# Second attention of a six-stage transformer kernel: GpSimd adds the key halves for all eight heads, and half of the output path moves by a slot

## The chip, the cores and the metric

The kernel runs on one core of one Trainium2 chip. The metric is the device time of one execution in microseconds (us). All of it is one launch; inputs and output lie in HBM.

## What is computed

The reference passes x (16 batches x 256 tokens x 128 channels, fp32) through six residual stages: a mixture-of-experts feed-forward, a grouped-query attention, the first feed-forward again, a routed feed-forward, a latent attention, and the routed feed-forward again. The change lies in the fifth, the second attention. Cut to what matters:

```python
c_q, c_kv = h_t @ W_DQ + b_DQ, h_t @ W_DKV + b_DKV      # 32 channels each
q = concat(c_q @ W_UQ + b_UQ, c_q @ W_QR + b_QR)        # 8 heads x (128 + 32)
k = concat(c_kv @ W_UK + b_UK, h_t @ W_KR + b_KR)
attn = softmax(q @ k.T / sqrt(160))                     # 256 x 256, per batch and head
out = (attn @ (c_kv @ W_UV + b_UV)) @ W_O + b_O
x = x + out                                             # h_t is layernorm(x)
```

## The kernel before

Each engine has its own hand-written list of instructions, and semaphores tie the lists together; the order inside a list never changes at run time. The functions `a1_pe`, `a1_act`, `a1_dve` and `a1_pool` issue the second attention for TensorE, ScalarE, VectorE and GpSimd. The first three loop over slots i = -2 to 15, and a slot has eight steps m = 0 to 7. In slot i three batches are in work at once:

- batch i + 2 is projected (`project`, lines 1139 to 1142, step 0), its keys are built by `head_keys` in two rounds of two (steps 2 and 4 on TensorE, lines 1158/1159), each copied to a rounded part by ScalarE (line 1315) and finished by VectorE (line 1397, one step later than the copy). TensorE's first round waits for VectorE's `low_inputs` (line 1386) and `vals` (line 1380). The second round reuses the same two PSUM banks and waits for VectorE's finished first round (semaphore kp_lo).
- batch i + 1 (from step 5 on, i + 2) gets its row maxima: in every step TensorE writes one bank of scores (`scores`, line 1176) and VectorE reduces it (`smax`, line 1404). There are two banks, so the scores of step m wait for the reduction of step m - 2.
- batch i gets its transposed scores (`scores_t`, line 1186) and exponentials (`exps`, ScalarE, line 1322). PT holds the exponentials: u = 0 for heads 0 to 3 (steps 0 to 3), u = 1 for heads 4 to 7 (steps 4 to 7), each with two halves of 128 keys.

The output path of a batch starts with `values(b, g)` (line 1201): 16 matmuls for the four heads of group g, two key halves each, into columns 0 to 255 of PSUM bank 6 + g. Beside it the sums over the keys go to columns 256 to 511 by matmuls with a block of ones (`sums`, line 1210). For g = 0 GpSimd first adds the two key halves (`pair`, line 1115, into PAIR), so that eight matmuls do; for g = 1 TensorE adds them with sixteen:

```python
if g:
    sums(b, g, (PT[:, g, 0, :, :], PT[:, g, 1, :, :]))
```

Then ScalarE copies the bank (`out_sums`, line 1328), TensorE turns it (`turn`, line 1221), VectorE divides (`normalise`, lines 1428/1429), TensorE turns both groups back (`back`, line 1227), ScalarE copies (`turned`, line 1333), TensorE projects out (`project_out`, line 1234), VectorE adds to the residual (`add`, line 1436) and takes the statistics (`stats`, lines 251/254), GpSimd makes the power (`next_power`, lines 261/263), VectorE normalises for the next stage (`normed`, line 270), TensorE turns it (`next_turn`, line 1243) and ScalarE copies it (`next_copy`, line 1337). VectorE's `maxima` (lines 1413 to 1416) packs the maxima of batch i + 1, TensorE turns them (line 1166), and VectorE's `shift` (line 1421) puts them into the queries. GpSimd also adds a bias to the residual (`bias`, line 1110).

Before the change slot i holds on TensorE: `turn(i-1, 0)` in step 0, `values` and sums of (i-1, 1) in step 1, `next_turn(i-2)` and `turn(i-1, 1)` in step 3, `values(i, 0)` and `back(i-1)` in step 5, the sums of (i, 0) and `maxima` in step 6, `project_out(i-1)` in step 7. A steady slot is one with all parts, i = 2 to 13: twelve of them.

## Time and profile before

| what | value |
|---|---|
| median of 3 runs (lowest, highest) | 1474.72 us (1471.44, 1475.7) |
| the profiled execution: its own time | 1477.36 us |
| its span, first to last instruction | 1475.6 us |
| TensorE matmul busy over the span | 1419.6 us (96%) |
| VectorE, ScalarE, GpSimd busy | 1113.8, 977.2, 633.1 us |
| mean granted TensorE clock | 0.99 |

Times in the trace count from the start of the span. A matmul row gives a modelled end, which overlaps the next one's start; the distance from start to start is what a group of matmuls costs. The twelve steady slots of the second attention lie from 1116.1 to 1285.9 us. Where a row merges several instructions (x16), its time is that of the whole group.

### The profile page before, as it was taken

How to read it: one execution, taken by the hardware profiler on the slowest of the kernel's cores; microseconds unless marked ns; L12 is line 12 of the kernel's file. 1: busy time of each engine (PE TensorE's matmuls, PEld its weight loads, DVE VectorE, ACT ScalarE, POOL GpSimd, SP SyncE). 2: the span in 40 equal slices, each digit the busy share in tenths (PEclk: the TensorE clock that was granted, in tenths of full speed). 3: DMA queues.
4: the chain of work that ended last, by engine and by line, in shares of the span. 5: the costliest groups of instructions: out<-in, count | busy, mean ns of one | idle time of the engine just before them, and what ended most of it. 6: DMA issues, size and time to landing. Idle time of an engine off the chain costs nothing.

```text
span 1475.6 us, 27285 instructions
## 1 busy us (share of the span) xinstructions
PE 1419.6 (96%) x9576; PEld 1146.5 (78%) x9576; DVE 1113.8 (75%) x2433; ACT 977.2 (66%) x1759; POOL 633.1 (43%) x596
## 2 busy tenths in 40 slices
PE   6999999989999999999999998999989999989998
PEld 6888888865666665688888876999967777769998
DVE  3766767688888889476777787687788898956765
ACT  5556656647777777755666567777746667657886
POOL 4466667610000000016666666677613233256664
PEclk8999999999999999999999999999999999989999
DMA  6000000000000000020000002000000000000001
GB/s 181 1 1 1 1 0 2 1 1 1 1 1 1 1 1 1 1 88 1 1 0 1 1 0 87 1 1 2 1 1 2 2 1 2 2 1 2 16 16 30
DMA packets 13319, 16.85 MB, mean 11 GB/s; under 512 B 768, under 2 KB 10496, under 8 KB 12928
## 3 DMA queue, kind: packets, MB, share of 16 engines
q1 hardware_dynamic: 13184, 15.11, 3.3%
q8 instruction: 77, 1.26, 0.3%
q14 instruction: 58, 0.48, 0.1%
HBM read 13.01 MB, written 2.10 MB: 10 GB/s over the span
## 4 chain that ended last, share of the span: by engine, by line
PE 84%; DVE 9%; ACT 3%; issue 2%; DMA 1%; POOL 0%; SPq 0%; DVEq 0%; POOLq 0%; ACTq 0%
PE PS L646 20%; PE PS L674 10%; PE PS L1835 9%; PE PS L1852 8%; PE PS L799 5%; PE PS L819 5%; PE PS L807 4%; PE PS L1201 2%; PE PS L778 2%; PE PS L1176 2%; PE PS L1210 2%; PE PS L1186 2%; PE PS L170 1%; PE PS L1158 1%; PE PS L1234 1%
## 5 line engine op out<-in xcount | busy, mean ns | idle before, releaser
L543 POOL TENSOR_TENSOR RR<-AR,RR 128x512 fp32r<-128x512 f32 x150 | 193.7, 1291 | 470.6 <-ACT RR L574 464.2
L610 ACT ACTIVATE AR<-PS 128x512 f32<-128x512 f32 x224 | 134.1, 599 | 164.7 <-PE PS L646 162.5
L512 DVE TENSOR_TENSOR AR<-AR,PS 128x512 f32<-128x512 f32 x224 | 153.4, 685 | 116.4 <-PE PS L646 113.7
L918 ACT ACTIVATE AR<-PS 128x512 f32<-128x512 f32 x256 | 152.4, 604 | 85.7 <-PE PS L807 85.0
L995 DVE TENSOR_REDUCE AR<-PS 128x2 f32<-128x512 f32 x256 | 172.2, 685 | 21.4 <-PE PS L799 20.6
L646 PE MATMUL PS<-XHI,WG 128*128 128x512 f32 x448 | 177.1, 395 | 0.0
L646 PE MATMUL PS<-XHI,WU 128*128 128x512 f32 x448 | 174.8, 390 | 0.9 <-DVE AR L512 0.7
L516 DVE TENSOR_TENSOR AR<-AR,PS 128x512 f32<-128x512 f32 x224 | 154.0, 687 | 8.1 <-POOL RR L543 0.5
L1835 PE MATMUL PS<-XHI,SL 128*128 128x256 f32 x576 | 135.0, 290 | 3.6 <-DVE XTR L2000 1.9
L2105 POOL CAST SL<-ZW 128x1024 fp32r x96 | 100.0, 1042 | 86.2 <-PE PS L1852 85.6
L1928 ACT ACTIVATE PS<-PS 128x1024 f32<-128x1024 f32 x96 | 96.9, 1009 | 59.5 <-PE PS L1835 59.2
L1835 PE MATMUL PS<-XLO,SL 128*128 128x256 f32 x576 | 133.9, 287 | 1.6 <-DVE XTR L2000 1.3
L799 PE MATMUL PS<-XLO,XHI 128*128 128x512 f32 x256 | 129.3, 505 | 3.0 <-DVE AR L995 2.4
L674 PE MATMUL PS<-RR,WD 128*128 128x512 f32 x450 | 126.5, 390 | 1.2 <-POOL RR L543 1.2
L2000 DVE SCALAR_TENSOR_TENSOR XTR<-PS,AR,RR 128x512 fp32r<-128x512 f32 x128 | 90.1, 746 | 45.5 <-ACT RR L1938 45.4
L1852 PE MATMUL PS<-XTR,SL 128*128 128x256 f32 x640 | 124.1, 284 | 0.3 <-DVE XTR L2000 0.3
L543 POOL TENSOR_TENSOR H<-AR,H 128x512 fp32r<-128x512 f32 x74 | 95.6, 1291 | 52.8 <-ACT H L574 50.8
L1322 ACT ACTIVATE AR<-PS 128x512 f32<-128x512 f32 x128 | 76.7, 603 | 46.8 <-PE PS L1186 46.1
L2103 POOL CAST SL<-ZW 128x1024 fp32r x96 | 99.9, 1041 | 16.4 <-DVE IDX L1764 6.8
L1852 PE MATMUL PS<-RR,SL 128*128 128x256 f32 x512 | 103.4, 285 | 2.3 <-DVE AR L1719 2.3
L1835 PEld LDWEIGHTS PS<-XHI,SL 128*128 128x128 f32 x576 | 100.6, 193 | 4.8 <-issue 3.8
L807 PE MATMUL PS<-XHI,XLO 128*128 128x512 f32 x256 | 102.9, 403 | 0.9 <-ACT AR L918 0.7
(284 smaller groups left out, 3510.0 us busy)
## 6 DMA issues: line engine op xcount, KB each, us to landing
X<-in_x SPq DMA_DIRECT2D x4, 512.0 KB, 6.5
out_x<-X SPq DMA_DIRECT2D x4, 512.0 KB, 3.5
AR<-in_w SPq DMA_DIRECT2D x1, 1792.0 KB, 11.7
XT<-in_w SPq DMA_DIRECT2D x1, 1608.0 KB, 6.3
AR<-in_zone_up SPq DMA_DIRECT2D x6, 256.0 KB, 5.2
AR<-in_zone_down SPq DMA_DIRECT2D x6, 256.0 KB, 6.1
XT<-in_sel SPq DMA_DIRECT2D x1, 896.0 KB, 6.5
SM<-in_small SPq DMA_DIRECT2D x1, 857.5 KB, 7.0
```

The costliest lines, as they stand in the source:

```text
L512: v.tensor_tensor(PRD[:, m % 2, :], SIL[:, m % 2, :], bank(2 + m % 2), ALU.mult).then_inc(S.prod, 1)
L516: v.tensor_tensor(GAT[:, m % 2, :], PRD[:, m % 2, :], bank(4 + m // SHARED), ALU.mult).then_inc(S.gated, 1)
L543: g.tensor_tensor(HL[k % 3], GAT[:, m % 2, :], HH[k % 3].bitcast(F32), ALU.subtract).then_inc(S.h_lo, 1)
L610: act.activation(SIL[:, m % 2, :], bank(m % 2), ACT.Silu).then_inc(S.silu, 1)
L646: last = pe.matmul(out, w[i][:, m * P:(m + 1) * P], x[:, bass.ds(c * 512, 512)], start=(j == 0), stop=(j == 2))
L674: last = pe.matmul(bank(6), WD[i][:, m, :], h[k % 3], start=(m == 0 and j == 0), stop=(m == MT0 - 1 and j == 2))
L799: pe.matmul(bank(m % 2), QS0[b % 3][:, j * SEQ + k * P:j * SEQ + (k + 1) * P], KS0[b % 3][:, 2 * gp:2 * gp + 2, :], start=True, stop=True) ...
L807: pe.matmul(bank(2 + m % 2), KS0[b % 3][:, g, k * P:(k + 1) * P], QS0[b % 3][:, jp * 512:(jp + 1) * 512], start=True, stop=True).then_inc( ...
L918: act.activation(PT[:, g % 2, k, 2 * jp:2 * jp + 2, :], bank(2 + m % 2).rearrange("p (j q) -> p j q", j=2), ACT.Exp, scale=SC0).then_inc(S ...
L995: v.tensor_reduce(MX[:, 2 * m:2 * m + 2], bank(m % 2).rearrange("p (h k) -> p h k", h=2), AX.X, ALU.max)\
L1835: last = pe.matmul(o, SL[:, k, 0, i, m * P:(m + 1) * P], x[:, b * SEQ:(b + 1) * SEQ], start=(j == 0), stop=(j == 2))
L1852: last = pe.matmul(bank(4 + b % 2)[:, 0:SEQ], SL[:, k, 1, i, m * P:(m + 1) * P], h[z % 3][:, at], start=(k == 0 and m == 0 and j == 0), st ...
```

## The change

GpSimd now forms PAIR for both groups of heads: `pair(b, u)` runs twice per batch, into the same buffer, and the second waits for the sums of the first (semaphore av). `values(b, g)` issues the values and, right behind them, eight matmuls of sums on PAIR; only the very last group (batch 15, g = 1) keeps sixteen. `pair_sums` is gone. On TensorE the even steps now hold everything: step 0 `project(i+2)`, `turn(i-1, 0)` and `project_out(i-2)`; step 2 `head_keys` and `values(i-1, 1)`; step 4 `head_keys`, `next_turn(i-2)`, `turn(i-1, 1)`; step 6 `back(i-1)`, `maxima(i+1)`, `values(i, 0)`. The odd steps hold scores and transposed scores alone. `project_out`, and with it everything behind it up to the residual, comes a slot later in name and about one step later in time. On VectorE `add(i-2)` moves from step 0 to step 1, behind the reduction and `normalise` and ahead of `low_inputs`; `stats` and `stacks` move to step 2; `normed` moves from step 1 to step 3, ahead of the two head-key instructions; `normalise(i-1, 1)` moves from step 4 to step 5.

```diff
--- before.py
+++ after.py
@@ -1109,16 +1109,18 @@
                 xs = X[:, b * TPB:(b + 1) * TPB, :]
                 g.tensor_tensor(xs, xs, CBB.unsqueeze(1).to_broadcast([P, TPB, H]), ALU.add).then_inc(S.xb, 1)
 
-            def pair(b):
-                g.wait_ge(S.exp, NS1 * b + 4)
-                wait(g, S.av, 2 * b - 1)
-                g.tensor_tensor(PAIR, PT[:, 0, 0, :, :], PT[:, 0, 1, :, :], ALU.add).then_inc(S.pair, 1)
+            def pair(b, u):
+                g.wait_ge(S.exp, NS1 * b + 4 * u + 4)
+                wait(g, S.av, 2 * b + u)
+                g.tensor_tensor(PAIR, PT[:, u, 0, :, :], PT[:, u, 1, :, :], ALU.add).then_inc(S.pair, 1)
 
             for i in range(-1, NB):
+                if i >= 1:
+                    pair(i - 1, 1)
                 if i >= 2:
                     next_power(g, n, i - 2)
                 if i >= 0:
-                    pair(i)
+                    pair(i, 0)
                 if i + 1 < NB:
                     bias(i + 1)
                 if i == NB - 2:
@@ -1200,8 +1202,11 @@
                     for j in range(4):
                         pe.matmul(o[32 * j:32 * j + 32, 0:SEQ], VA1[:, b % 4, k, :], PT[:, g, k, j, :],
                                   start=(k == 0), stop=(k == 1), skip_group_check=True)
-                if g:
+                if (b, g) == (NB - 1, 1):
                     sums(b, g, (PT[:, g, 0, :, :], PT[:, g, 1, :, :]))
+                else:
+                    pe.wait_ge(S.pair, 2 * b + g + 1)
+                    sums(b, g, (PAIR,))
 
             def sums(b, g, parts):
                 o = bank(6 + g)
@@ -1210,10 +1215,6 @@
                         last = pe.matmul(o[32 * j:32 * j + 32, SEQ:2 * SEQ], ones[:, 0:32], part[:, j, :],
                                          start=(k == 0), stop=(k == len(parts) - 1), skip_group_check=True)
                 last.then_inc(S.av, 1)
-
-            def pair_sums(b):
-                pe.wait_ge(S.pair, b + 1)
-                sums(b, 0, (PAIR,))
 
             def turn(b, g):
                 pe.wait_ge(S.os, 2 * b + g + 1)
@@ -1269,24 +1270,22 @@
                         Z.next_turn(NB - 2)
                     if m == 3 and i == -1:
                         Z.next_turn(NB - 1)
-                    if m == 1 and done:
+                    if m == 0 and done:
+                        turn(i - 1, 0)
+                    if m == 0 and gone:
+                        project_out(i - 2)
+                    if m == 2 and done:
                         values(i - 1, 1)
-                    if m == 3 and gone:
+                    if m == 4 and gone:
                         next_turn(i - 2)
-                    if m == 3 and done:
+                    if m == 4 and done:
                         turn(i - 1, 1)
-                    if m == 5 and now:
-                        values(i, 0)
-                    if m == 5 and done:
+                    if m == 6 and done:
                         back(i - 1)
-                    if m == 6 and now:
-                        pair_sums(i)
                     if m == 6 and next_:
                         maxima(i + 1)
-                    if m == 0 and done:
-                        turn(i - 1, 0)
-                    if m == 7 and done:
-                        project_out(i - 1)
+                    if m == 6 and now:
+                        values(i, 0)
 
             Z = ZTAIL["pe"]
             project(0)
@@ -1339,7 +1338,7 @@
             def step(i):
                 now, far, done, gone = (0 <= i + d < NB for d in (0, 2, -1, -2))
                 for m in range(NS1):
-                    if m == 2 and done:
+                    if m == 3 and done:
                         out_sums(i - 1, 1)
                     if m == 7 and now:
                         out_sums(i, 0)
@@ -1353,12 +1352,12 @@
                     if m == 2 and far:
                         head_keys(i + 2, 0)
                         head_keys(i + 2, 1)
-                    if m == 4 and gone:
+                    if m == 5 and gone:
                         next_copy(i - 2)
                     if m == 4 and far:
                         head_keys(i + 2, 2)
                         head_keys(i + 2, 3)
-                    if m == 6 and done:
+                    if m == 7 and done:
                         turned(i - 1)
                     if i == NB - 2 and m in (1, 3, 5, 7):
                         early_high(n + 1, m // 2)
@@ -1452,12 +1451,14 @@
                         smax(b, s)
                     if m == 1 and done:
                         normalise(i - 1, 0)
-                    if m == 0 and gone:
+                    if m == 1 and gone:
                         add(i - 2)
-                        stats(i - 2)
                     if m == 1 and far:
                         low_inputs(i + 2)
                         vals(i + 2)
+                    if m == 2 and gone:
+                        stats(i - 2)
+                    if m == 2 and far:
                         stacks(i + 2)
                     if m == 1 and i == -2:
                         Z.next_copy(NB - 3)
@@ -1472,11 +1473,11 @@
                         Z.normed(NB - 1)
                     if m == 4 and i == -1:
                         Z.next_copy(NB - 1)
-                    if m == 1 and gone:
+                    if m == 3 and gone:
                         normed(i - 2)
                     if m == 4 and next_:
                         maxima(i + 1)
-                    if m == 4 and done:
+                    if m == 5 and done:
                         normalise(i - 1, 1)
                     if m == 3 and far:
                         head_keys(i + 2, 0)
@@ -1874,6 +1875,7 @@
             if resident:
                 A = TAIL["pe"]
                 A.turn(NB - 1, 0)
+                A.project_out(NB - 2)
                 A.values(NB - 1, 1)
                 up(0)
                 A.turn(NB - 1, 1)
```

How it moves the instructions, at two places. Line numbers of the changed kernel (1178 is the old 1176, 1188 the old 1186, 1160 the old 1158, 1203 the old 1201, 1215 the old 1210, 1222 the old 1221, 1235 the old 1234, 1403 the old 1404, 1427 and 1428 the old 1428 and 1429, 1435 the old 1436, 1385 the old 1386).

TensorE, steady slot, from the turn of step 0 to the first head keys of step 2. Before:

```order
L1139 MATMUL PS<-XF,SM 128x256 [waits a1_qs2,a1_kp_lo,next_xt]
L1140 MATMUL PS<-XF,SM 128x256
L1142 MATMUL PS<-SM,XF 128x32 x2
L1221 MATMUL PS<-SM,AR 128x128 [waits a1_os]
L1221 MATMUL PS<-SM,AR 128x128 x3
L1176 MATMUL PS<-XTR,XLO 128x512 [waits a1_smax]
L1186 MATMUL PS<-XLO,XTR 128x256 [waits a1_exp]
L1186 MATMUL PS<-XLO,XTR 128x256
L1201 MATMUL PS<-AR,SM 32x256 [waits a1_x_new,a1_exp]
L1201 MATMUL PS<-AR,SM 32x256 x7
L1210 MATMUL PS<-AR,SM 32x256 x8
```

And now:

```order
L1222 MATMUL PS<-SM,AR 128x128 [waits a1_os]
L1222 MATMUL PS<-SM,AR 128x128 x3
L1235 MATMUL PS<-SM,XN 128x128 [waits a1_aot]
L1235 MATMUL PS<-SM,XN 128x128 x3
L1178 MATMUL PS<-XTR,XLO 128x512 [waits a1_smax]
L1188 MATMUL PS<-XLO,XTR 128x256 [waits a1_exp]
L1188 MATMUL PS<-XLO,XTR 128x256
L1178 MATMUL PS<-XTR,XLO 128x512 [waits a1_smax]
L1188 MATMUL PS<-XLO,XTR 128x256 [waits a1_exp]
L1188 MATMUL PS<-XLO,XTR 128x256
L1160 MATMUL PS<-RR,BSA 128x256 [waits a1_v,a1_kl]
```

Between the scores of step 1 (the first row of 1178 here) and the first head keys (1160) there stood 32 matmuls of values and sums; now there stand two pairs of scores and nothing else. `project_out` stands ahead of the scores of step 1.

VectorE, steady slot, from the reduction of step 1 to the head keys of step 3. Before:

```order
L1404 TENSOR_REDUCE AR<-PS 128x2 [waits a1_s_pe]
L1428 RECIPROCAL AR<-PS 128x8 [waits a1_aot_pe,a1_ot]
L1429 TENSOR_TENSOR AR<-PS,AR 128x256 [waits a1_r_chain]
L1386 SCALAR_TENSOR_TENSOR RR<-PS,SM,RR 64x256 [waits a1_kp_pe,a1_qh]
L1380 TENSOR_TENSOR SM<-PS,SM 128x64 [waits a1_av,a1_kv]
L1392 SCALAR_TENSOR_TENSOR XLO<-XLO,SM,XN 128x256 [waits a1_st_pe,a1_qh]
L270 TENSOR_SCALAR XN<-X,LN 128x128 [waits next_tr,next_rstd]
L270 TENSOR_SCALAR XN<-X,LN 128x128
L1404 TENSOR_REDUCE AR<-PS 128x2 [waits a1_s_pe] x2
L1397 SCALAR_TENSOR_TENSOR XLO<-XLO,SM,PS 128x512 [waits a1_st_pe,a1_kp_hi] x2
L1404 TENSOR_REDUCE AR<-PS 128x2 [waits a1_s_pe]
```

And now, beginning with the reductions of steps 7, 0 and 1:

```order
L1403 TENSOR_REDUCE AR<-PS 128x2 [waits a1_s_pe] x3
L1427 RECIPROCAL AR<-PS 128x8 [waits a1_aot_pe,a1_ot]
L1428 TENSOR_TENSOR AR<-PS,AR 128x256 [waits a1_r_chain]
L1435 TENSOR_TENSOR X<-X,PS 128x256 [waits a1_xb,a1_out]
L1385 SCALAR_TENSOR_TENSOR RR<-PS,SM,RR 64x256 [waits a1_kp_pe,a1_qh,a1_x_new]
L1379 TENSOR_TENSOR SM<-PS,SM 128x64 [waits a1_av,a1_kv]
L1403 TENSOR_REDUCE AR<-PS 128x2 [waits a1_s_pe]
L251 BN_STATS STAT<-X 128x6 x2
L254 BN_AGGR LN<-STAT 128x2 [waits next_chain]
L254 BN_AGGR LN<-STAT 128x2
L1391 SCALAR_TENSOR_TENSOR XLO<-XLO,SM,XN 128x256 [waits a1_st_pe,a1_qh]
L1403 TENSOR_REDUCE AR<-PS 128x2 [waits a1_s_pe]
```

The residual add (1435) now stands between the reduction of step 1 and the low inputs (1385) for which TensorE's head keys wait; the two rows of line 270 left this place and stand, in the changed kernel, behind the reduction of step 3 and directly ahead of the head-key rows.

## Rows read from the trace of the kernel before

**Rows 1.** Windows: busy us of each engine in two stretches, with granted clock (PEclk)
```profile
core 0: us, PE busy (x) PEld busy (x) DVE busy (x) ACT busy (x) POOL busy (x), PEclk, DMA share, GB/s
1074.00:1098.00 24.00, 17.36 (x110) 14.72 (x109) 20.96 (x47) 10.75 (x21) 3.20 (x4) 1.00 0.00 1
1182.00:1196.00 14.00, 13.90 (x129) 10.69 (x128) 12.46 (x30) 9.40 (x21) 3.90 (x5) 1.00 0.01 1
```

**Rows 2.** Timeline of TensorE, steady slot: start us, duration us, line, operation, count
```profile
1184.72 0.64 PE L1210 MATMUL PS<-RRF,SM 128*32 128x256 f32 x8
1185.30 0.44 PE L1166 MATMUL PS<-SM,AR 128*128 128x128 f32 x2
...
1186.89 0.48 PE L1176 MATMUL PS<-XTR,XLO 128*128 128x512 f32 x1
...
1189.05 0.48 PE L1176 MATMUL PS<-XTR,XLO 128*128 128x512 f32 x1
...
1189.70 1.07 PE L1201 MATMUL PS<-AR,SM 128*32 128x256 f32 x16
1190.59 1.05 PE L1210 MATMUL PS<-AR,SM 128*32 128x256 f32 x16
1191.56 0.50 PE L1176 MATMUL PS<-XTR,XLO 128*128 128x512 f32 x1
...
1192.14 0.28 PE L1158 MATMUL PS<-RR,BSA 128*128 128x256 f32 x1
...
1193.08 0.40 PE L1176 MATMUL PS<-XTR,XLO 128*128 128x512 f32 x1
...
1194.92 0.38 PE L1158 MATMUL PS<-RR,BSA 128*128 128x256 f32 x1
```

**Rows 3.** Timeline of VectorE, the same slot; in brackets idle us before, and releaser
```profile
1188.01 0.41 DVE L1436 TENSOR_TENSOR X<-X,PS 128x256 f32<-128x256 f32 x1
...
1189.57 0.69 DVE L1404 TENSOR_REDUCE AR<-PS 128x2 f32<-128x512 f32 x1 [0.35 <-PE PS L1176]
1190.18 0.20 DVE L1428 RECIPROCAL AR<-PS 128x8 f32<-128x8 f32 x1
...
1190.75 0.47 DVE L1386 SCALAR_TENSOR_TENSOR RR<-PS,SM,RR 64x256 fp32r<-64x256 f32 x1
...
1191.67 0.59 DVE L270 TENSOR_SCALAR XN<-X,LN 128x128 f32<-128x128 f32 x2
1192.18 0.68 DVE L1404 TENSOR_REDUCE AR<-PS 128x2 f32<-128x512 f32 x1
...
1194.12 1.40 DVE L1397 SCALAR_TENSOR_TENSOR XTR<-XLO,SM,PS 128x512 fp32r<-128x512 f32 x2
```

**Rows 4.** Timeline of TensorE, slot 0, which has no values in its step 1
```profile
1094.06 0.36 PE L1158 MATMUL PS<-RR,BSA 128*128 128x256 f32 x1 [1.01 <-DVE SM L1380]
...
1096.92 0.38 PE L1158 MATMUL PS<-RR,BSA 128*128 128x256 f32 x1 [0.72 <-DVE XTR L1397]
```

**Rows 5.** Timeline of VectorE, slot 0, low inputs
```profile
1093.31 0.48 DVE L1386 SCALAR_TENSOR_TENSOR RR<-PS,SM,RR 64x256 fp32r<-64x256 f32 x1 [0.23 <-ACT XLO L1310]
```

**Rows 6.** Timeline of GpSimd, pair of one slot and of the next
```profile
1180.32 2.39 POOL L1115 TENSOR_TENSOR RRF<-AR 128x1024 f32<-128x1024 f32 x1 [4.15 <-ACT AR L1322]
...
1194.48 2.38 POOL L1115 TENSOR_TENSOR RRF<-AR 128x1024 f32<-128x1024 f32 x1 [4.15 <-ACT AR L1322]
```

**Rows 7.** Timeline of ScalarE, the exponential just before the second of these pairs
```profile
1193.78 0.62 ACT L1322 ACTIVATE AR<-PS 128x512 f32<-128x512 f32 x1
```

**Rows 8.** Timeline of VectorE, two small scalings of slot 15
```profile
1303.19 1.98 DVE L1727 TENSOR_SCALAR AR<-AR 10x8 f32<-10x8 f32 x1
...
1305.83 0.22 DVE L1741 TENSOR_SCALAR AR<-AR 10x8 f32<-10x8 f32 x1
```

**Rows 9.** Timeline of GpSimd, pair of slot 15
```profile
1302.79 2.36 POOL L1115 TENSOR_TENSOR RRF<-AR 128x1024 f32<-128x1024 f32 x1 [1.93 <-ACT AR L1322]
```

**Rows 10.** Timeline of TensorE, slot 15
```profile
1307.00 1.12 PE L1227 MATMUL PS<-SM,AR 128*128 128x128 f32 x4 [1.82 <-DVE AR L1429]
```

## The prediction

> **What bounds the kernel now.** I read the share of busy time first, then busy time by windows, then the timelines of one steady slot on each engine, then slot 0, and last the order of the changed kernel. In a steady slot TensorE is busy 13.90 of 14.00 us at full clock, VectorE 12.46, ScalarE 9.40, GpSimd 3.90 [rows 1]. The slot's length is 14.16 us, from one pair on GpSimd to the next [rows 6]. So TensorE's work sets the time, with VectorE only about 1.5 us behind it: a change here is worth what it takes off TensorE only as long as VectorE's results still arrive before TensorE asks for them. Two such meetings matter. The first head keys need VectorE's low inputs and values bias, which stand behind the reduction of the scores of step 1. The second round of head keys needs VectorE's finished first round, which stands behind the reduction of step 3. The reader should see that at the second meeting there is no room left: from the scores of step 3 (1193.08) to the head keys (1194.92) pass 1.84 us [rows 2], and VectorE's part starts at 1194.12, is half of 1.40 us long and so ends 0.10 us before TensorE goes on [rows 3]. TensorE's own work between the two is about 1.6 us (estimate: 1.84 less the short stop), so it already waits 0.23 us. At the first meeting there is room: from the scores of step 1 (1189.05) to the head keys (1192.14) TensorE has 3.09 us [rows 2], of which the values and sums take 1.86 (1189.70 to 1191.56).
>
> **Slot 0 shows what happens without that cover.** It has no values and sums in step 1 and no output path. There TensorE stood still for 1.01 us at the first head keys and 0.72 us at the second round, each time until VectorE was done [rows 4]. The change moves the cover away in all twelve steady slots.
>
> **What is removed.** Eight of the sixteen sum matmuls per slot: sixteen took 0.97 us (1190.59 to 1191.56), eight 0.58 (1184.72 to 1185.30) [rows 2], so 0.39 us. Besides, values and sums now follow each other directly and the 32-bit steps stand together in the even steps, so TensorE changes less often between kinds of matmul. I put that at 0.45 us (estimate; a pair of scores and transposed scores took 0.65 us ahead of the values, 1189.05 to 1189.70, and 0.58 ahead of the head keys [rows 2], and there are several such places). TensorE's work falls by 0.84 us; bounds 0.39 (the eight matmuls alone) and 1.1.
>
> **What GpSimd gets.** A second addition of 2.39 us [rows 6]; with it GpSimd is busy about 6.3 of 14 us. The pair of heads 4 to 7 can start after the exponentials of step 7 and is wanted in step 2 of the next slot, over 5 us later; the pair of heads 0 to 3 starts after step 3's exponentials and is wanted at the end of step 6, again over 5 us later, against 2.4. Neither is waited for in a steady slot: priced at nothing, covered by that distance; if the cover were gone TensorE would stop for what is missing of 2.4 us. The wait for the first sums ahead of the second pair is met long before. The power computation is queued behind the second pair, and its statistics come later still.
>
> **What is moved, and what it costs.** All four terms are a wait, as VectorE's chain less TensorE's own way. Two pairs of scores with nothing else are about 1.05 us on TensorE (0.58 [rows 2] for the first, slightly less for the second).
>
> 1. First head keys. From the scores of step 1: 0.52 to the reduction's start, 0.61 for it, 0.57 for reciprocal and division (to 1190.75) [rows 2, 3], 0.45 for the residual add that now stands there (0.41 [rows 3] and its start), and 0.75 from the low inputs' start to the head keys (1093.31 to 1094.06) [rows 4, 5]. Sum 2.90, TensorE's way 1.05, wait 1.85. Part of it comes from `project_out` standing ahead of these scores, so that VectorE idles through a step 0 of some 3 us and cannot begin earlier.
> 2. Second head keys. The chain was 1.84; `normed` now stands in it, 0.51 us (1191.67 to 1192.18) [rows 3], and the scores come 0.1 later behind sums. Sum 2.45, less 1.05: wait 1.40. Its cover is `turn` and `next_turn`, which now stand behind the head keys.
> 3. `back` in step 6 waits for `normalise(i-1, 1)`, now behind the reduction of step 5: 0.52 + 0.61 and about 0.7 for the division (estimate from 0.57 to the next operation [rows 3] and the hand-over), 1.83, less 1.05: 0.78.
> 4. `maxima` waits for the third head-key copy, which follows that division on VectorE: from the division's start 0.34 + 0.70 + 0.10, against TensorE's 0.48 + 0.41: 0.25. Upper bound 0.7 (a whole copy), lower 0.
>
> Waits 4.28, of which 0.23 was there before; less 0.84 of work: **+3.2 us per steady slot**, which becomes 17.4 us. Twelve slots: +38.4. Slot 0 puts values and sums behind `maxima`, +1.1; slot 1 has terms 1 and 2 without the add and `normed`, +1.3; slot 14 +0.5. In slot 15 VectorE's division of batch 14 comes behind one more routing pick and `values(15, 0)` behind `back`, where TensorE already waited 1.82 us [rows 10]: +3.9. Ends +6.8 (estimate, bounds 0 and 12). `project_out(14)` only changes places at the very end, with nothing between. Sum +45.2. The profiled execution took 1477.4 us (span 1475.6), so 1522.6 there; it lay 2.6 us above the median of the runs, 1474.7, so **1520 us**.
>
> **A shared resource, weighed.** VectorE's scaling of 10x8 elements took 1.98 us at 1303.19, where one of the same size took 0.22 at 1305.83 [rows 8]; it ended at 1305.17, and the pair on GpSimd ended at 1305.15 (1302.79 + 2.36) [rows 9]. So a scaling that begins beside a pair is held until the pair is done. `normed` is two scalings. The pair started 1.40 us after the scores of step 3 (1193.08 to 1194.48), 0.70 after the exponential [rows 6, 7]. In the new order the reduction would free VectorE for the first scaling 1.04 us after those scores (where the head keys started [rows 2, 3]), and the second would start at 1.30. It is ahead by 0.1 us, so I charge nothing; the other outcome is rival A.
> The Trainium skill (SBUF — State Buffer, section Who interferes with whom) calls this an exclusive lock held for a whole instruction by whichever of the two engines issues first. The row agrees for a GpSimd operation that came first; by the rule the order of my 0.1 us would give 1520, and the reverse order the time of rival A.
>
> **Rivals.**
> A. *The second scaling of `normed` is caught by the pair.* It then starts at 3.78 instead of 1.30 us after the scores, and the head keys with it: +2.45 per slot, in twelve slots +29, so 1550 us. For it: the margin is 0.1 us. Against: the scaling is ahead in my working. Some slots could go either way.
> B. *Milder.* The waits overlap more than my fixed chains allow, or TensorE's work falls by 1.1: half of the 38, some 1498 to 1507.
> C. *Faster.* TensorE's saving comes out and VectorE's results arrive in time: 12 x (0.84 + 0.23) = 13, so 1462 us. It decides where VectorE's chain from the scores to the head keys falls below 1.05 us. Against: the reduction and its start alone are 1.13, and slot 0 stood still at both places.
> D. *No gain, no loss*: VectorE's waits just eat the saving, 1475; needs waits of 1.1 us in all, and term 2 alone is 1.4.
> E. *TensorE's clock falls* in the gaps. Slots -1 and 0 were busy for 17.36 of 24 us (72%) at clock 1.00 [rows 1], and a new slot would be busy 13.1 of 17.4 (75%). At half the clock a slot would be some 26 us, the total past 1600. Only the end of the stage risks some of it.
> The change not doing what it says is excluded by its order: eight sum matmuls on PAIR stand behind both groups' values.
>
> **How the numbers follow.** Forecast 55%, A 23%, B 12%, C 5%, D 3%, E 2%. About 0.3% (4.4 us) is what a measurement of this kernel can tell from no change. Faster 0.05, same 0.03, slower 0.92. The range runs from B's low end, 1498, to 1555, A with longer ends; it leaves out C, D, E and some of the edges of A.
>
> **What would show it.** In the profile after: the distance from one first pair to the next about 17.4 us (A: 19.8); TensorE idle ahead of line 1160 until VectorE, 1.7 to 1.8 us for the first and 1.2 to 1.3 for the second head keys; idle ahead of line 1228 (`back`) of 0.6; VectorE idle over 2 us ahead of the reduction of step 1; no idle time ahead of line 1215 until GpSimd; the scalings of line 270 at 0.33 us each (A: one of them near 2.7). A slot below 14 us would make me wrong altogether; one near 15.5 would say that my chains are too rigid.

## The result and the profile after

| | before | after |
|---|---|---|
| median (lowest, highest), 4 runs each | 1475.21 us (1471.44, 1476.27) | 1560.88 us (1558.23, 1563.55) |
| ratio, 95% interval | | 1.0586 (1.0558 to 1.0613) |
| span of the profiled execution | 1475.6 us | 1557.8 us |
| mean granted TensorE clock | 0.99 | 0.978 |

Slower by 5.9%, 41 us above the forecast and 6 us above the range. The page of the changed kernel, busy time and the group of the additions:

```profile
PE 1433.8 (92%) x9456; PEld 1158.2 (74%) x9456; DVE 1133.1 (73%) x2433; ACT 980.3 (63%) x1759; POOL 671.5 (43%) x611
...
L1115 POOL TENSOR_TENSOR RRF<-AR 128x1024 f32<-128x1024 f32 x31 | 73.0, 2356 | 116.6 <-ACT AR L1321 116.6
```

GpSimd has its 31 additions (16 before). TensorE is busy for 14 us more than before (1419.6) although it has fewer matmuls to do, and is idle on top of that. The list of waits of TensorE over the second attention shows where; these are its first four rows (before, the same list of the steady slots is empty). Columns: engine and what waited, releaser, us in total, times, longest:

```profile
PE PS L1160 <- DVE XTR L1396: 24.7, 8, 3.4
PE PS L1160 <- DVE SM L1379: 20.5, 12, 1.7
PE PS L1160 <- DVE XLO L1396: 11.2, 4, 3.4
PE PS L1228 <- DVE AR L1428: 7.4, 6, 4.1
```

In all four rows TensorE waits for VectorE. Stops of 3.4 us stand beside stops of 1.7 us at the same line, 1160, the head keys. The distance from one first addition on GpSimd to the next is the slot [rows 6: 14.16 before]. Windows of such slots, with the granted clock in the third column from the right:

```profile
core 0: us, PE busy (x) PEld busy (x) DVE busy (x) ACT busy (x) POOL busy (x), PEclk, DMA share, GB/s
1130.29:1147.77 17.48, 13.91 (x120) 10.72 (x120) 12.07 (x31) 9.88 (x21) 6.56 (x6) 1.00 0.00 1
...
1169.08:1189.46 20.38, 15.16 (x120) 11.98 (x120) 14.20 (x32) 9.87 (x21) 6.50 (x5) 0.92 0.01 2
1209.85:1232.74 22.89, 17.57 (x120) 13.47 (x120) 14.37 (x32) 9.87 (x21) 6.51 (x6) 0.78 0.00 1
1312.30:1332.10 19.80, 13.91 (x120) 10.72 (x120) 14.21 (x32) 9.88 (x21) 6.51 (x6) 1.00 0.00 1
```

The first slot is 17.48 us, as forecast (17.4). The last is 19.80 at the same clock, the slot of rival A (19.8). The two between them are longer still, and their clock is below 1.00. Here is the last one on TensorE, from the scores of its step 3:

```profile
1310.85 0.50 PE L1178 MATMUL PS<-XTR,XLO 128*128 128x512 f32 x1
...
1315.43 0.39 PE L1160 MATMUL PS<-RR,BSA 128*128 128x256 f32 x1 [3.37 <-DVE XLO L1396]
...
1318.03 0.40 PE L1188 MATMUL PS<-XLO,XTR 128*128 128x256 f32 x2
1319.15 0.66 PE L1228 MATMUL PS<-SM,AR 128*128 128x128 f32 x4 [0.72 <-DVE AR L1428]
1319.89 0.41 PE L1168 MATMUL PS<-SM,AR 128*128 128x128 f32 x2
...
1326.01 0.40 PE L1188 MATMUL PS<-XLO,XTR 128*128 128x256 f32 x2
1328.12 0.36 PE L1160 MATMUL PS<-RR,BSA 128*128 128x256 f32 x1 [1.71 <-DVE SM L1379]
```

The first head keys stop it for 1.71 us, `back` for 0.72, and the second head keys, the second row, for 3.37. The same slot on VectorE, then on GpSimd:

```profile
1312.00 2.72 DVE L270 TENSOR_SCALAR XN<-X,LN 128x128 f32<-128x128 f32 x2
1314.64 1.40 DVE L1396 SCALAR_TENSOR_TENSOR XLO<-XLO,SM,PS 128x512 fp32r<-128x512 f32 x2
```

```profile
1312.30 2.34 POOL L1115 TENSOR_TENSOR RRF<-AR 128x1024 f32<-128x1024 f32 x1 [1.61 <-ACT AR L1321]
```

The group of line 270, `normed`, takes 2.72 us instead of 0.59 [rows 3]. It ends (1312.00 + 2.72 = 1314.72; 1314.64 is when the next starts) with the addition, 1312.30 + 2.34 = 1314.64. This is the hold of [rows 8, 9], and line 1396, for which TensorE waits, stands behind it. In the 13 slots from 2 to 14 `normed` was held so in 11. One where it was not, VectorE and then GpSimd and TensorE:

```profile
1232.28 0.59 DVE L270 TENSOR_SCALAR XN<-X,LN 128x128 f32<-128x128 f32 x2
1232.78 1.40 DVE L1396 SCALAR_TENSOR_TENSOR XTR<-XLO,SM,PS 128x512 fp32r<-128x512 f32 x2
```

```profile
1232.74 2.37 POOL L1115 TENSOR_TENSOR RRF<-AR 128x1024 f32<-128x1024 f32 x1 [3.21 <-ACT AR L1321]
```

```profile
1230.83 0.80 PE L1178 MATMUL PS<-XTR,XLO 128*128 128x512 f32 x1
...
1232.10 0.40 PE L1188 MATMUL PS<-XLO 128*128 128x256 f32 x2
1233.58 0.39 PE L1160 MATMUL PS<-RR,BSA 128*128 128x256 f32 x1 [1.08 <-DVE XTR L1396]
```

Here the first scaling starts 0.46 us ahead of the addition (1232.28, 1232.74), in the held slot 0.30 (1312.00, 1312.30). The scores ahead of it take 0.80 us where they take 0.50 in the held slot: the granted clock is 0.50 from 1228.5 to 1231.5, and from the scores to the addition pass 1.91 us (1230.83 to 1232.74) instead of 1.45 (1310.85 to 1312.30), to the first scaling 1.45 instead of 1.15. The other free slot looks the same (scores 0.80 us long at 1128.35, scaling at 1129.80, addition at 1130.29). So the two slots that escaped the hold are those whose step 3 met the lower clock. A view of VectorE whose edge falls between the two scalings shows the second of a held group alone; then its addition on GpSimd:

```profile
1147.72 2.47 DVE L270 TENSOR_SCALAR XN<-X,LN 128x128 f32<-128x128 f32 x1
```

```profile
1147.77 2.34 POOL L1115 TENSOR_TENSOR RRF<-AR 128x1024 f32<-128x1024 f32 x1 [1.60 <-ACT AR L1321]
```

The second scaling has its start on record 0.05 us ahead of the addition and is held all the same: to 1150.19, where the addition ends at 1150.11 and the next operation starts. Right behind that hold TensorE's rows look like this:

```profile
1150.90 0.58 PE L1160 MATMUL PS<-RR,BSA 128*128 128x256 f32 x1 [3.37 <-DVE XTR L1396]
1151.28 0.42 PE L1161 MATMUL PS<-RR,BSB 128*128 128x256 f32 x1
```

0.58 and 0.42 us where the same two rows behind the stop of 1315.43 take 0.39 and 0.28: from 1150 to 1155 the granted clock is 0.50, the lower of TensorE's two levels, 1.2 GHz. The mean clock was below 1.00 in eight of the nine held slots between 1130.29 and 1353.42 (0.78 to 0.92), counted from addition to addition, and in neither of the two free ones.

**The sum over eleven slots.** From 1130.29 to 1353.42 are 223.1 us, before 11 x 14.15 = 155.7: +67.5. Order: 11 x (17.49 - 14.15) = 36.7. Hold: nine slots x (19.80 - 17.49) = 20.8. Clock: the nine held slots took 188.2 us, at full clock 9 x 19.80 = 178.2: 9.9. Of the whole +82.2 us of span, 14.7 lie outside, where the twelfth slot and the ends are; the clock was lower in some of these too (0.91, 0.90 and 0.89 in the windows of slots 1, 13 and 14). Rows of the ends, TensorE, slots 14 and 15:

```profile
1373.79 0.44 PE L1244 MATMUL PS<-SM,XN 128*128 128x128 f32 x2 [2.72 <-DVE XN L270]
...
1385.15 0.64 PE L1215 MATMUL PS<-RRF,SM 128*32 128x256 f32 x8 [1.36 <-POOL RRF L1115]
...
1392.27 1.12 PE L1228 MATMUL PS<-SM,AR 128*128 128x128 f32 x4 [4.12 <-DVE AR L1428]
```

1373.79 is again the held `normed`. `back` of slot 15 waited 1.82 us before [rows 10] and now 4.12.

### The profile page after: what moved, and what is told of

Same layout as the page of the kernel before. It is cut to its first block, busy times and chain, and to the rows that moved or that the text cites. A ratio compares the mean times of both kernels' runs of the same rounds, so it can differ in the third digit from the quotient of the medians.

```text
span 1557.8 us, 27076 instructions
## 1 busy us (share of the span) xinstructions
PE 1433.8 (92%) x9456; PEld 1158.2 (74%) x9456; DVE 1133.1 (73%) x2433; ACT 980.3 (63%) x1759; POOL 671.5 (43%) x611
## 3 DMA queue, kind: packets, MB, share of 16 engines
q8 instruction: 76, 1.25, 0.3%
## 4 chain that ended last, share of the span: by engine, by line
PE 78%; DVE 12%; issue 4%; ACT 4%; POOL 1%; DMA 1%; SPq 0%; DVEq 0%; POOLq 0%; ACTq 0%
PE PS L646 19%; PE PS L674 9%; PE PS L1836 8%; PE PS L1853 8%; PE PS L799 5%; PE PS L819 4%; PE PS L807 4%; DVE XN L270 2%; PE PS L1203 2%; PE PS L778 2%; PE PS L1178 2%; PE PS L1160 1%; PE PS L170 1%; PE PS L1215 1%; PE PS L1222 1%
## 5 line engine op out<-in xcount | busy, mean ns | idle before, releaser
L610 ACT ACTIVATE AR<-PS 128x512 f32<-128x512 f32 x224 | 134.0, 598 | 164.8 <-PE PS L646 162.6
L918 ACT ACTIVATE AR<-PS 128x512 f32<-128x512 f32 x256 | 152.3, 603 | 85.8 <-PE PS L807 85.0
L995 DVE TENSOR_REDUCE AR<-PS 128x2 f32<-128x512 f32 x256 | 172.1, 685 | 21.6 <-PE PS L799 20.6
L1403 DVE TENSOR_REDUCE AR<-PS 128x2 f32<-128x512 f32 x128 | 86.3, 685 | 86.2 <-PE PS L1178 86.0
L2107 POOL CAST SL<-ZW 128x1024 fp32r x96 | 100.3, 1045 | 85.7 <-PE PS L1853 85.2
L1115 POOL TENSOR_TENSOR RRF<-AR 128x1024 f32<-128x1024 f32 x31 | 73.0, 2356 | 116.6 <-ACT AR L1321 116.6
```

The source lines that it names most:

```text
L610: act.activation(SIL[:, m % 2, :], bank(m % 2), ACT.Silu).then_inc(S.silu, 1)
L918: act.activation(PT[:, g % 2, k, 2 * jp:2 * jp + 2, :], bank(2 + m % 2).rearrange("p (j q) -> p j q", j=2), ACT.Exp, scale=SC0).then_inc(S ...
L995: v.tensor_reduce(MX[:, 2 * m:2 * m + 2], bank(m % 2).rearrange("p (h k) -> p h k", h=2), AX.X, ALU.max)\
```

## The experiments

Medians of the kernel before lay at 1472.5, 1473.0 and 1472.1 us in the first three batches (e1 to e4, e5 to e8, e9 and e10) and at 1473.1 in the last (e11, e12). Ratios are against these. The spans quoted are those of the one profiled execution of each kernel.

### e1: the hold taken out

The first pair waits for one more exponential, so it starts later than both scalings. All else is the changed kernel.

```diff
-                g.wait_ge(S.exp, NS1 * b + 4 * u + 4)
+                g.wait_ge(S.exp, NS1 * b + 4 * u + 5 - u)
```

> The changed kernel, with one number altered: the pair of heads 0 to 3 waits for five exponentials of its batch instead of four, so that it starts some 0.5 us later. Theory (a lock: the second scaling of normed is held by the pair in 11 of 13 slots): no scaling of line 270 over 0.7 us within the slots, every steady slot near 17.5 us, the time 25 to 40 us below the changed kernel's 1560.9, so 1521 to 1536. Rival (the excess over my forecast is TensorE's lowered clock or GpSimd's second addition as such): the same number of pairs, the same gaps apart from the lock, so less than 10 us gained.

Measured: 1532.5 us, ratio 1.0406 (1.0374 to 1.0437), span 1526.8, clock 0.994. VectorE, then GpSimd, then the waits of TensorE:

```profile
1201.23 0.59 DVE L270 TENSOR_SCALAR XN<-X,LN 128x128 f32<-128x128 f32 x2
```

```profile
1202.02 2.38 POOL L1115 TENSOR_TENSOR RRF<-AR 128x1024 f32<-128x1024 f32 x1 [2.10 <-ACT AR L1321]
```

```profile
PE PS L1160 <- DVE SM L1379: 17.1, 10, 1.7
PE PS L1228 <- DVE AR L1428: 7.9, 10, 1.3
```

No `normed` is held in the steady slots, the slot is 17.67 us (1184.35 to 1202.02), and none of their stops is above 1.7 us. So hold and clock together are worth 31.0 us of span (1557.8 to 1526.8), or 28.4 by the medians (1560.88 to 1532.5; the profiled execution was the fastest of e1's four). That is near the 20.8 + 9.9 of the windows, which hold nine of the eleven held slots. The order of the instructions is worth the other 51.2 of span: in slots 12 x (17.67 - 14.15) = 42.2, and 9.0 for the rest, of which 1.6 is one slot of 19.24 us (1237.35 to 1256.59, clock 0.91). The addition now meets the cast of `maxima` (0.66 us at 1203.77, 0.17 where nothing holds it), which TensorE does not feel: `back` waits 0.72 us (1206.25), as in the changed kernel.

### e2 and e3: one part of the change alone, `normed` late

Kernel before, `normed` moved to step 3 ahead of the head keys on VectorE, `next_turn` to step 4 on TensorE. e3 also delays the pair as e1 does.

```diff
-                    if m == 1 and gone:
+                    if m == 3 and gone:
                         normed(i - 2)
...
-                    if m == 3 and gone:
+                    if m == 4 and gone:
                         next_turn(i - 2)
```

> The kernel before, with one part of the change alone: VectorE's normed in step 3 ahead of the head keys instead of step 1, and next_turn accordingly in step 4 ahead of TensorE's head keys. Theory: the chain to the second head keys grows by the 0.51 us of normed and the scaling is caught by the pair, 2.4 us more; a steady slot goes from 14.15 to about 17.1 us, the time to about 1475 + 35 = 1510. Rival (chain alone, no lock in the old order): 14.7 us and about 1481.

> As the run before (normed late in the kernel before), and the pair waits for five exponentials instead of four. Theory: the lock goes and the chain term stays: a steady slot of 14.6 to 14.7 us, time about 1481. Rival (the pair start does not matter): as the run before.

e2: 1482.81 us, ratio 1.0061 (1.0039 to 1.0084). A miss: nothing was held in the steady slots. VectorE and GpSimd:

```profile
1209.55 0.59 DVE L270 TENSOR_SCALAR XN<-X,LN 128x128 f32<-128x128 f32 x2
```

```profile
1209.91 2.48 POOL L1115 TENSOR_TENSOR RRF<-AR 128x1024 f32<-128x1024 f32 x1 [4.15 <-ACT AR L1322]
```

The first scaling leads the addition by 0.36 us (1209.55, 1209.91), so the second starts some 0.10 ahead and wins; this time the addition is the longer one, 2.48 instead of 2.38 us. Between the 0.30 to 0.31 of the held steady slots and this 0.36 lies the lead of the first scaling at which it is decided. The slot is 14.55 us (1195.36 to 1209.91), so this part of the change by itself costs 0.40 a slot, VectorE's chain to the second head keys. In slot 14 alone `normed` was held: its two scalings took 2.62 us from 1294.92, the addition 2.34 from 1295.12, and TensorE stopped for 2.30 us at `next_turn` (1297.59). This is part of what the total has above 12 x 0.40 = 4.8 us.

The rows of e2 also show where the lead comes from. The scores of step 3 start at 1208.50, the first scaling 1.05 us later and the addition 1.41, which are the 1.04 and 1.40 of the prediction. In the changed kernel (1310.85, above) they are 1.15 and 1.45. There these scores stand behind sums; in e2, as in the kernel before, they stand behind head keys.

e3: 1485.92 us, ratio 1.0086 (1.0058 to 1.0115), and slower than e2 where no difference, or a gain, was expected. The addition now meets the cast of `maxima`:

```profile
1215.95 1.09 DVE L1413 CAST RR<-AR 128x16 fp32r<-128x16 f32 x1
```

It takes 1.09 us (0.32 in e2), and `back`, which waits for the division behind it, stops TensorE for 0.4 us a slot; the slot is 15.01 us (1199.60 to 1214.61). An addition of 2.4 us that is moved away from one VectorE operation lands on another.

### e4: the other part alone, both pairs on GpSimd

Kernel before with the second pair and eight sums less, the order of everything else kept.

```diff
-                if g:
+                if (b, g) == (NB - 1, 1):
                     sums(b, g, (PT[:, g, 0, :, :], PT[:, g, 1, :, :]))
+                elif g:
+                    pe.wait_ge(S.pair, 2 * b + 2)
+                    sums(b, g, (PAIR,))
```

> The kernel before, with the other part of the change alone: GpSimd adds the halves for all eight heads, values and sums of heads 4 to 7 stay in step 1, everything else where it was. Theory (the addition itself is harmless and the order did the damage): eight matmuls fewer, 0.39 us per slot off TensorE, none waited for; slot 13.8 us, time about 1469 (1465 to 1473). Rival (GpSimd's second addition hurts by itself, by the lock or by TensorE waiting for it in step 1): 1480 or more, with idle time ahead of line 1210 or VectorE instructions held.

Measured: 1468.88 us (1466.67 to 1470.42, 10 runs), ratio 0.997 (0.9956 to 0.9984): faster than both kernels, by 3.6 us than before (a small gain, but its interval leaves out 1, and e12 shows it again) and by 92 than after. TensorE's sums:

```profile
1188.16 0.61 PE L1215 MATMUL PS<-RRF,SM 128*32 128x256 f32 x8
1188.70 0.50 PE L1178 MATMUL PS<-XTR,XLO 128*128 128x512 f32 x1
```

The slot is 13.71 us (additions of GpSimd at 1191.62 and 1205.33), 0.45 less than 14.16; TensorE's list of waits over the steady slots is empty. The sums take 0.54 us (1188.16 to 1188.70) where sixteen took 0.97. So the second addition on GpSimd, which the change is named for, is its good part, and what costs 90 us is the order that came with it. That is by difference: the new order without the second addition was not run. Twelve slots would give 5.4 us, the runs gave 3.6; e11 looks for the rest.

### e5 and e6: the two waits at the head keys, one at a time, on e1

e5 puts VectorE's low inputs and values bias ahead of the reduction of step 1. e6 puts the first round of head keys ahead of the reduction and `normed` of step 3.

```diff
+                    if m == 1 and far:
+                        low_inputs(i + 2)
+                        vals(i + 2)
                     if 0 <= b < NB:
                         smax(b, s)
...
-                    if m == 1 and far:
-                        low_inputs(i + 2)
-                        vals(i + 2)
```

```diff
+                    if m == 3 and far:
+                        head_keys(i + 2, 0)
+                        head_keys(i + 2, 1)
                     if 0 <= b < NB:
                         smax(b, s)
...
-                    if m == 3 and far:
-                        head_keys(i + 2, 0)
-                        head_keys(i + 2, 1)
```

> The changed kernel with the late pair (no lock), and VectorE's low inputs and values bias ahead of the reduction of step 1 instead of behind reduction, division and residual add. Theory (the first head keys wait for VectorE's chain, 1.85 us): that wait goes; values(i-1, 1) then waits about 0.4 us for the residual add. Steady slot 17.67 - 1.45 = 16.2 us, time about 1532 - 17 = 1515 (1509 to 1520). Rival (TensorE would stand still there for something else, such as ScalarE's projection copies): less than 5 us gained.

> The changed kernel with the late pair, and VectorE's first two head-key instructions ahead of the reduction of step 3 and of normed. Theory: term 2 (1.4 us at the second head keys) goes, but the cast of maxima then begins while the late pair runs and is held until its end, so that back waits 0.6 us longer: steady slot 17.67 - 0.8 = 16.9 us, time about 1523. Rival (no holding of the cast, terms simply add): 16.3 us and 1515.

e5: 1507.82 us, ratio 1.0235 (1.0216 to 1.0254). The slot falls from 17.67 to 16.08 us (1197.20 to 1213.29 on GpSimd), and the wait for line 1379 is gone from the list: 1.59 us a slot for the first term, a little more than expected. `values` of heads 4 to 7 now wait 0.3 us a slot for the residual add, as expected. Twelve slots make 19.1 us; the spans fell by 17.3 (1526.8 to 1509.5), the medians by 24.7. The two profiled executions were the fastest of e1's four and the slowest of e5's, so the two differences are apart by the spread of the runs. The median is 1 us below the expected 1509 to 1520.

e6: 1536.91 us, ratio 1.0445 (1.042 to 1.047): no gain at all, where 1523 was expected. Its wait at the second head keys is gone, but VectorE reaches the cast of `maxima` during the addition:

```profile
1206.56 2.04 DVE L1412 CAST RR<-AR 128x16 fp32r<-128x16 f32 x1
```

```profile
1206.20 2.37 POOL L1115 TENSOR_TENSOR RRF<-AR 128x1024 f32<-128x1024 f32 x1 [3.73 <-ACT AR L1321]
```

```profile
1210.24 0.66 PE L1228 MATMUL PS<-SM,AR 128*128 128x128 f32 x4 [2.24 <-DVE AR L1428]
```

The cast is held for 2.04 us, to 1208.60, and the addition ends at 1208.57; `back` then stops TensorE for 2.24 instead of 0.72 us. At full clock the slot is 17.48 us (1225.32 to 1242.80), 0.19 less than in e1: nearly all that is won at the second head keys is lost again at `back`. In three of the eleven slots from 1133.04 to 1331.82 the clock was lower as well (0.84, 0.91, 0.91) and the slot longer: 20.71 us, 19.12 (the one of the rows, 1206.20 to 1225.32) and 19.07. The same lock, another place. I had seen the direction and put too small a price on it, and none on the clock.

### e7 and e8: further than e4

e8 is e4 with the head keys of step 3 ahead of the reduction (the diff of e6), to take away the 0.23 us at the second head keys. e7 has besides the sums of (i, 0) right behind `values(i, 0)`; the diff is this part, against e4.

```diff
-                elif g:
-                    pe.wait_ge(S.pair, 2 * b + 2)
+                else:
+                    pe.wait_ge(S.pair, 2 * b + g + 1)
                     sums(b, g, (PAIR,))
...
-                    if m == 6 and now:
-                        pair_sums(i)
```

> The kernel before with both pairs (as the run of both pairs), values(i, 0) in step 5 directly followed by its sums, and VectorE's first two head-key instructions ahead of the reduction of step 3. Theory: the 0.23 us stop at the second head keys goes, values and sums without a switch between save 0.3 us: slot 13.71 - 0.5 = 13.2 us, time about 1462. Rival (VectorE, 12.7 us busy per slot, becomes the bound or the pair is late for the sums in step 5): 13.7 us or more.

> The kernel before with both pairs and only the head-key instructions moved ahead of the reduction of step 3. Theory: the 0.23 us stop and the cold start of some 0.1 us behind it go: slot 13.4 us, time about 1465. Rival: the stop comes back elsewhere, slot 13.7 us, 1469.

e7: 1469.53 us, ratio 0.9981 (0.9971 to 0.999); e8: 1469.98, 0.9977 (0.9965 to 0.9988). Both slots are 13.72 us in the mean of eleven, the same as e4's, so the rivals of both expectations came true and not the 13.2 and 13.4. The listed stops of e7 are at `maxima` now (line 1168, 0.2 to 0.3 us a slot), those of e8 at `back` (0.5 us a slot). VectorE does the same work in the same time between two of its results; whichever stands first, TensorE meets the other one late. That is my reading of where the stops moved; no run tests it by itself.

### e9 and e10: the order of the change with VectorE put right

e9: the changed kernel with low inputs, values bias and add ahead of the reduction of step 1, the head keys ahead of reduction and `normed` in step 3, and the first pair waiting for `maxima`'s last operation too, so that it can hold neither scaling nor cast. e10 also has, in step 5, `normalise` and head keys ahead of the reduction. The diff is part of e10's: the delay of the addition, and step 5; steps 1 and 3 move as in e5 and e6, with the add besides.

```diff
                 g.wait_ge(S.exp, NS1 * b + 4 * u + 4)
+                if u == 0 and b + 1 < NB:
+                    g.wait_ge(S.mm, b + 2)
...
+                    if m == 5 and done:
+                        normalise(i - 1, 1)
+                    if m == 5 and far:
+                        head_keys(i + 2, 2)
+                        head_keys(i + 2, 3)
                     if 0 <= b < NB:
                         smax(b, s)
```

> The changed kernel with three edits against my terms: on VectorE in step 1 low inputs, values bias and residual add ahead of the reduction, in step 3 the first head keys ahead of the reduction and of normed; on GpSimd the pair of heads 0 to 3 starts only after maxima has been packed, so that it holds neither normed nor the cast. Theory (order on VectorE and the lock are the whole damage; terms 3 and 4, 0.8 and 0.25 us, stay): steady slot 14.2 to 14.5 us, time 1480 to 1486. Rival (the one-slot delay or GpSimd's second addition costs by itself): above 1495, with waits at other places.

> As the run before, and in step 5 VectorE's division and second head keys ahead of the reduction as well. Theory: terms 3 and 4 go too, and the new order gives back what its shorter TensorE work promises: steady slot 13.1 to 13.5 us, below the kernel before's 14.15, with the ends of the stage 9 us dearer; time 1466 to 1474, so faster than the kernel before or equal. Rival (VectorE at 12.7 us per slot becomes the bound): slot 13.8 us or more, 1478 and above.

e9: 1492.15 us, ratio 1.0132 (1.0117 to 1.0148), slot 15.12. e10: 1482.36, ratio 1.0064 (1.005 to 1.0078), slot 14.27. The changed kernel was 85.7 us above the kernel before, e10 is 10.2 above it in its own batch: about 75 us are recovered by the order on VectorE and the start of one addition alone, with TensorE's list unchanged. But both stayed above what was expected (1480 to 1486 and 1466 to 1474), and e10 above the kernel before; e10's slot is in the range of its rival (13.8 us or more). What is left of stops in e10, on TensorE:

```profile
1196.34 0.40 PE L1190 MATMUL PS<-XLO 128*128 128x256 f32 x2
1196.80 0.39 PE L1162 MATMUL PS<-RR,BSA 128*128 128x256 f32 x1
...
1198.57 0.44 PE L1246 MATMUL PS<-SM,XN 128*128 128x128 f32 x2 [0.38 <-DVE XN L270]
...
1199.98 0.40 PE L1190 MATMUL PS<-XLO 128*128 128x256 f32 x2
1200.30 0.66 PE L1230 MATMUL PS<-SM,AR 128*128 128x128 f32 x4
1201.05 0.41 PE L1170 MATMUL PS<-SM,AR 128*128 128x128 f32 x2
```

```profile
1199.82 0.42 DVE L1430 TENSOR_TENSOR AR<-PS,AR 128x256 f32<-128x256 f32 x1
1200.16 0.74 DVE L1398 SCALAR_TENSOR_TENSOR XTR<-XLO,SM,PS 128x512 fp32r<-128x512 f32 x1
```

The rows of the second fence are VectorE's, the division and the first half of the third head keys. Counted from start to start: transposed scores to head keys 0.46 us where 0.24 are usual (0.22 too many); head keys to `next_turn` 0.66 (1197.91 to 1198.57) where 0.12 are usual, as 1234.70 to 1234.82 in the changed kernel (0.54); `back` 0.06 behind the division's end (1199.82 + 0.42), 0.32 instead of 0.24 behind the scores (0.08); `maxima` 0.75 behind `back` instead of 0.41 (0.34). That is 1.18 us of stops, of which the list shows 0.38. The one at `maxima` it does not show at all, but `maxima` waits for the third head keys by the code, and started 0.15 behind their end (1200.16 + 0.74 to 1201.05) here and 0.14 behind it in the changed kernel (1237.16 + 0.74 to 1238.04) and in e1 (1206.11 + 0.74 to 1206.99). That it is this wait is argued from the three, not tested by itself. VectorE's results still come late, each by a little, at four places.

TensorE's own work in e10 is then 14.27 - 1.18 = 13.09 us. The kernel before has two stops, the 0.23 known ahead and one at `back` that I had not seen: 1197.81, again 0.06 behind the end of the division (1197.33 + 0.42), and 1.10 behind the values, which take 0.89 [rows 2: 1189.70 to 1190.59] (0.21). So its own work is 14.16 - 0.44 = 13.72, that of e4, with the same two stops, 13.71 - 0.24 - 0.23 = 13.24. The eight matmuls are worth 0.48 us, and the new grouping another 0.15.

### e11 and e12: what e4 loses at its end

e12 is e4 again, beside e11, in which batch 14 keeps its sixteen sums and GpSimd makes no addition for them. In e4 this addition stood behind four router additions of 4.99 us that are issued ahead of it in slot 14.

```diff
-                if (b, g) == (NB - 1, 1):
+                if g and b >= NB - 2:
                     sums(b, g, (PT[:, g, 0, :, :], PT[:, g, 1, :, :]))
...
-                if i >= 1:
+                if 1 <= i < NB - 1:
                     pair(i - 1, 1)
```

> Both pairs as in e4, but the last but one batch (14, g = 1) keeps its sixteen sum matmuls and GpSimd makes no addition for it. In e4 that addition stood in GpSimd's queue behind the four early router additions of line 1678 (4.99 us, from 1288.99), began only at 1293.94, and TensorE's sums waited 2.03 us for it at 1296.34. Theory queue (that wait is why twelve slots at -0.45 = -5.4 us gave only -3.6): the wait is gone, eight matmuls (0.43 us) come back, so 1.6 us faster than e4: about 3.5% of a per cent less in ratio terms 0.001, i.e. 1467.3 where e4 has 1468.9, ratio 0.996, slot 15 without a stop at line 1215. Rival (slot 15 has other waits that take its place: back for VectorE's division, 1.6 us in e4): same time as e4, and the stop at line 1232 of slot 15 grows by what line 1215 lost.

> The kernel of e4 once more, on the same chip as e11, so that the two can be compared directly: 1468.9, slot 13.71, a stop of 2.0 us at line 1215 in slot 15.

e11: 1467.46 us (1465.68 to 1471.6, 9 runs), ratio 0.9967 (0.9954 to 0.9981). e12: 1468.78, ratio 0.9975 (0.9965 to 0.9985). GpSimd and then TensorE in e12:

```profile
1287.33 4.99 POOL L1678 TENSOR_TENSOR XHI<-XF,XLO 128x512 fp32r<-128x512 f32 x4
1292.28 2.34 POOL L1115 TENSOR_TENSOR RRF<-AR 128x1024 f32<-128x1024 f32 x1
```

```profile
1294.67 0.64 PE L1215 MATMUL PS<-RRF,SM 128*32 128x256 f32 x8 [2.02 <-POOL RRF L1115]
```

TensorE's 2.02 us at the sums are gone in e11. From the values of slot 14 to the last values that wait for the residual are 20.08 us there (1285.43 to 1305.51) and 22.23 in e12 (1285.48 to 1307.71), so 2.15 less; the stop at `back` in slot 15 grew only from 1.61 to 1.82. The medians differ by 1.3 us with intervals that overlap; the spans, 1463.9 and 1466.1, say the same with 2.2. e11 has the lowest median of the study, 5.6 us below the kernel before in the same batch, though these runs do not part it from e12 for certain.

## Why the prediction was wrong where it was, and right where it was

**The direction and the cause were right.** TensorE lost its cover at the two places that the prediction named, and waits for VectorE there.

**The waits, term by term.** A listed stop begins at the modelled end of the last matmul; from start to start, less what is usual, is the true cost. (1) First head keys: forecast 1.85; measured 2.11 - 0.24 = 1.87 (1326.01 to 1328.12), and e5 won 1.59 of it back; the other 0.3 us are what `values` then waited. (2) Second head keys, not held: forecast 1.40; 1.48 - 0.24 = 1.24 in the changed kernel (1232.10 to 1233.58). (3) `back`: forecast 0.78; 1.12 - 0.24 = 0.88 (1318.03 to 1319.15). (4) `maxima`: forecast 0.25; 0.74 - 0.41 = 0.33 (1319.15 to 1319.89), unlisted, see e10. Together 4.28 forecast, 4.32 found.

**The two smaller numbers beside them.** Taken off for what was there already: 0.23, in truth 0.44, since `back` waited too. TensorE's saving: 0.84, in truth 13.72 - (17.48 - 4.32) = 0.56; the eight matmuls gave the 0.4 to 0.5 expected, the 0.45 for grouping came out at 0.1. Two errors of opposite sign, and the slot of 17.48 stood against 17.4.

**The step that failed: "It is ahead by 0.1 us, so I charge nothing."** The lead of the second scaling over the addition was 1.40 - 1.30 us, counted from the scores of step 3 in the order of the kernel before. Term 2 of the same prediction adds 0.1 us because in the new order these scores "come 0.1 later behind sums"; the lead leaves it out. In the changed kernel the first scaling stands 1.15 us behind the scores instead of 1.04 and the addition 1.45 instead of 1.40 (1310.85, 1312.00, 1312.30), and the second scaling was 0.05 us ahead (1147.72, 1147.77), which was not enough. In e2, where the scores stand behind head keys as before, the forecast 1.04 and 1.40 came true (1.05 and 1.41) and nothing was held in the steady slots. Rival A, given 23%, happened in 11 of 13 slots, with 2.3 us (forecast 2.45). Its 19.8 us slot fits to the digit partly by luck: 17.48 + 2.31 instead of 17.35 + 2.45, and only one of the nine held slots had it, the others met a lower clock on top. The trace agrees with the Trainium skill (SBUF — State Buffer, section Who interferes with whom) in that one of the two engines is held to the end of the other's instruction, and in e2 the addition was the one held, by 0.1 us. What the recorded starts do not show is who issued first: the loser at 1147.72 has the earlier one.

**The second miss: rival E was no rival but a companion of A.** Rival A's 1550 was made at full clock. With a stop of 3.4 us in it the clock was lower in eight of nine slots, 9.9 us in eleven slots; with stops of 1.7, 1.1 to 1.25 and 0.7 us in a slot it stayed at 1.00 in both free slots and in ten of the eleven steady slots of e1 from 1131.35 to 1327.09, and with the 2.2 us of e6 in eight of eleven. Why the one held slot was spared, and one of e1's was not, no run shows. With A's 29 and about 10 for the clock the forecast would have been 1559.

The clue stood in the trace of the kernel before. Its cast of `maxima` on VectorE, and the division behind it:

```profile
1196.16 0.74 DVE L1413 CAST RR<-AR 128x16 fp32r<-128x16 f32 x1
...
1197.33 0.42 DVE L1429 TENSOR_TENSOR AR<-PS,AR 128x256 f32<-128x256 f32 x1
```

The cast ends at 1196.90, the addition at 1194.48 + 2.38 = 1196.86 [rows 6]. A cast of this size is 0.17 us where nothing holds it (1316.67 in the changed kernel). The cast takes 0.74 us in the steady slots looked at (1111.26 to 1210.30, eight of them). So they already paid 0.57 us of hold, and `back`, behind it, waited 0.21 (that the one makes the other is argued, no run takes it out), and I looked for the hold only in slot 15.

**The ends:** forecast 6.8, in e1 9.0 less the 1.6 of its slow slot, 7.4. `back` of slot 15 was the largest stop there (4.27 us in e1), as said.

**Priced at nothing:** right for the second addition in the steady slots (e4: no wait for it in any). Wrong at the end, where it stands behind GpSimd's router additions: 1.36 us in the changed kernel (1385.15), 2.0 in e4.

## What to carry to other kernels

Before an operation of the busiest engine is moved, look at which results of the next busiest engine it gave time to, and move the queue of that engine with it: the same TensorE order cost 1560.9 or 1482.4 us depending on VectorE's and on the start of one addition. A long GpSimd operation and a VectorE operation of the kind that can be held, whose starts fall within 0.1 us of each other by your working, are not a free pair: make the sum with the hold in it, and where that gives stops like the 3.4 us seen here, with the lower clock too. An allowance made in one term (the 0.1 us for scores behind sums) belongs in every margin that counts from the same point. And try the parts of a change alone: the part that its first words name was a gain of 0.3%, the rest of it a loss of 6%.

## What the runs showed that I had not expected

- Of two operations that start 0.05 us apart (1147.72 and 1147.77), the one with the later recorded start had the lock; at about 0.10 us, in e2, the earlier one had it. I have no run that looks between, and none that tells whether it is recorded start or something ahead of it that decides.
- A cast of 128x16 elements is held too, 2.04 us instead of 0.17; the head keys of line 1396, whose other operand lies in PSUM, ran beside an addition at their usual 1.40 (1232.78 beside 1232.74).
- A wait of some tenths need not show in the list of waits. Of the 1.18 us of stops in e10's slot it had 0.38; the distance from start to start, held against the same pair of rows elsewhere, shows the rest.
- The lower clock also let two slots go free: there the addition started late enough for the second scaling to be some 0.2 us ahead of it.
- How much the hold alone would cost without the clock's fall was not run by itself; 20.8 and 9.9 are from windows.
